# Moving the causal mask of a two-pass attention from TensorE to VectorE's maximum and to GpSimd's probabilities

## What is computed

```python
# x is (1, 2048, 512); 16 heads of 32
qkv = (x @ W_qkv + b_qkv).reshape(B, S, 16, 96).transpose(0, 2, 1, 3)
q, k, v = jnp.split(qkv, 3, axis=-1)
scores = jnp.einsum('bhqd,bhkd->bhqk', q, k) / np.sqrt(32)
scores = jnp.where(causal, scores, -10000.0)      # causal: key <= query
probs = jax.nn.softmax(scores, axis=-1)
ctx = jnp.einsum('bhqk,bhkd->bhqd', probs, v)
```

## Time and profile before

| | |
|---|---|
| median of three runs | 2159.66 us (2156.12 to 2161.9) |
| the profiled execution | 2161.04 us, span 2159.3 us |
| TensorE busy | 2000.4 us, 93% of the span |
| VectorE busy | 1098.8 us, 51% |
| ScalarE busy | 638.9 us, 30% |
| GpSimd busy | 436.7 us, 20% |
| mean granted TensorE clock | 0.956 |
| the attention block | from 195.3 us to about 873 us of the span |

### The profile page before, as it was taken

The page is one execution under the profiler, slowest core; times in us unless marked ns, Lnnn a source line. Parts: engine busy times, 40 slices in busy tenths (PEclk is TensorE's granted clock), DMA queues, the critical chain, the costliest instruction groups (busy, mean ns, idle before and its releaser), DMA issues. The chain is left out here.

```text
span 2159.3 us, 25676 instructions
## 1 busy us (share of the span) xinstructions
PE 2000.4 (93%) x10088; PEld 1415.3 (66%) x10088; DVE 1098.8 (51%) x1908; ACT 638.9 (30%) x1152; POOL 436.7 (20%) x385
## 2 busy tenths in 40 slices
PE   6997799999999999769999999997999869999998
PEld 4675444445444543557888888886887548888886
DVE  4452586677676760664434344334543674344334
ACT  3221144545545556231111111112321232111111
POOL 1124245756564345400000000000000300000000
PEclk9998599999999999979999999999999989999999
DMA  8625331151231100310000000002000002010002
GB/s 306 214 98 149 77 71 39 28 121 42 50 79 32 32 2 1 127 64 30 30 30 30 1 30 30 1 1 79 12 6 10 20 0 79 20 30 10 15 1 78
DMA packets 61720, 111.86 MB, mean 52 GB/s; under 512 B 6000, under 2 KB 21248, under 8 KB 61568
## 3 DMA queue, kind: packets, MB, share of 16 engines
q1 hardware_dynamic: 54144, 85.05, 14.0%
q0 software_dynamic: 7456, 25.18, 3.9%
HBM read 84.77 MB, written 25.44 MB: 51 GB/s over the span
## 5 line engine op out<-in xcount | busy, mean ns | idle before, releaser
L858 DVE TENSOR_REDUCE part_max<-banks 128x1 f32<-128x512 f32 (+2 forms) x640 | 356.4, 613 | 179.9 <-PE banks L734 109.0
L838 ACT ACTIVATE probs<-banks 128x512 f32<-128x512 f32 (+3 forms) x640 | 310.8, 538 | 362.0 <-PE banks L765 194.5
L734 PE MATMUL banks<-kst,qst 96*128 96x512 f32 (+2 forms) x640 | 276.0, 450 | 35.7 <-DVE part_max L858 20.2
L761 PE MATMUL banks<-qst,kst 98*128 98x512 f32 (+2 forms) x640 | 263.7, 423 | 13.9 <-DMA qst<-max_dram 12.3
L1312 DVE TENSOR_TENSOR tokens_a<-banks,tokens_a 128x512 f32<-128x512 f32 x224 | 151.6, 688 | 72.0 <-PE banks L216 70.3
L734 PEld LDWEIGHTS banks<-kst,qst 96*128 96x128 f32 x640 | 132.9, 210 | 82.3 <-DVE part_max L858 57.9
L761 PEld LDWEIGHTS banks<-qst,kst 98*128 98x128 f32 x640 | 125.8, 197 | 86.3 <-issue 54.1
L214 PE MATMUL banks<-h_hi,f_wg_hi 128*128 128x512 f32 x432 | 170.4, 395 | 12.1 <-DVE f_wg_lo L1276 12.1
L1337 DVE TENSOR_TENSOR tokens_b<-banks,tokens_b 128x512 f32<-128x512 f32 x64 | 44.3, 692 | 267.3 <-ACT tokens_b L1258 267.3
L214 PE MATMUL banks<-f_d_hi,f_hid_hi 128*128 128x512 f32 x432 | 171.1, 396 | 5.9 <-issue 3.6
L215 PE MATMUL banks<-h_lo,f_wg_hi 128*128 128x512 f32 x432 | 169.9, 393 | 0.0
(11 more groups left out here) (189 smaller groups left out, 3271.0 us busy)
## 6 DMA issues: line engine op xcount, KB each, us to landing
tokens_a<-in_L_wmod SPq DMA_DIRECT2D x12, 1024.0 KB, 6.9
qst<-q_hi SPq DMA_DIRECT2D x32, 256.0 KB, 5.9
kst<-k_hi SPq DMA_DIRECT2D x32, 256.0 KB, 8.4
tokens_b<-in_L_attn_x SPq DMA_DIRECT2D x4, 1024.0 KB, 13.2
q_hi<-qk_out_hi POOLq DMA_DIRECT2D x16, 256.0 KB, 3.4
q_lo<-qk_out_lo POOLq DMA_DIRECT2D x16, 256.0 KB, 3.4
k_hi<-qk_out_hi POOLq DMA_DIRECT2D x16, 256.0 KB, 3.1
k_lo<-qk_out_lo POOLq DMA_DIRECT2D x16, 256.0 KB, 3.4
```

The costliest lines, as they stand in the source:

```text
L734: mm = nc.tensor.matmul(dst[:, 0:wide], qst[0:BIASROW, n % QS, h, P * t:P * t + P], kst[0:BIASROW, (NB * g + c) % KS, h, 0:wide], start=Tr ...
L761: mm = nc.tensor.matmul(dst[:, c0:512], kst[0:BIASROW + 2, ck % KS, h, at:at + P], qst[0:BIASROW + 2, n % QS, h, c0:512], start=True, stop ...
L838: nc.scalar.activation(probs[:, q % PS, h, c0:512], bank[3 + sh % 3][:, c0:512], ACT.Exp, scale=SCALE).then_inc(exp_done, 1)
L858: nc.vector.tensor_reduce(part_max[:, n % 2, ht, c:c + 1], bank[slot % 3][:, 0:wide], AX_X, ALU.max).then_inc(max_read, 1)
```

## The change

The 512 mask matmuls are gone, and the bf16 tables with them. In the first pass, a diagonal max tile is reduced by one fused call that adds a mask `later` (SBUF, 640 columns, its window shifted by the tile) to the scores in place and keeps the maximum; it becomes two instructions on VectorE, the fused one and one that writes out the accumulator. In the second pass the later keys get whatever exponential they get, and GpSimd sets them to zero in `probs` with an affine select: 128 instructions of two heads by 128 columns, four a diagonal step. The context of a diagonal step waits for these. The butterflies of a pair are split, rounds 0 and 1 behind the first diagonal step's selects, rounds 2 and 3 and the store behind the second's. `later` is loaded on SyncE's queue behind the first pair's queries and keys (128 KB), and the load of constants at the start is 256 KB smaller.

```diff
                         wide = 512 if c < j else max(P * (t + 1), 2 * P)
-                        mm = nc.tensor.matmul(dst[:, 0:wide], qst[0:BIASROW, n % QS, h, P * t:P * t + P],
-                                              kst[0:BIASROW, (NB * g + c) % KS, h, 0:wide],
-                                              start=True, stop=(c < j))
-                        if c == j:
-                            at = P * t
-                            mw = 2 * P if t == 0 else P
-                            mm = nc.tensor.matmul(dst[:, at:at + mw], ident16[:], mask_queries[:, 0:mw],
-                                                  start=False, stop=True)
-                        mm.then_inc(max_mm, 1)
+                        nc.tensor.matmul(dst[:, 0:wide], qst[0:BIASROW, n % QS, h, P * t:P * t + P],
+                                         kst[0:BIASROW, (NB * g + c) % KS, h, 0:wide],
+                                         start=True, stop=True).then_inc(max_mm, 1)
...
-                        if t >= 0:
-                            mw = 2 * P if t == 3 else P
-                            mm = nc.tensor.matmul(dst[:, c0:c0 + mw], ident16[:], mask_keys[:, 2 * P - mw:2 * P],
-                                                  start=False, stop=True)
...
-                            pe.wait_ge(exp_done, 4 * q + 4)
+                            if diagonal:
+                                pe.wait_ge(masked, masks_before(s) + 2 * half + 2)
+                            else:
+                                pe.wait_ge(exp_done, 4 * q + 4)
...
-                        nc.vector.tensor_reduce(part_max[:, n % 2, ht, c:c + 1], bank[slot % 3][:, 0:wide], AX_X,
-                                                ALU.max).then_inc(max_read, 1)
+                        scores = bank[slot % 3][:, 0:wide]
+                        if c == j:
+                            at = P * (TB - 1 - t)
+                            nc.vector.tensor_tensor_reduce(out=scores, in0=scores, in1=later[:, at:at + wide], scale=1.0,
+                                                           scalar=LOWEST, op0=ALU.add, op1=ALU.max,
+                                                           accum_out=part_max[:, n % 2, ht, c:c + 1]).then_inc(max_read, 1)
...
+                    def mask(s):
+                        n, i = steps[s]
+                        for half in range(2):
+                            q, c0 = 2 * s + half, P * (2 * i + half - TB * (n % NB))
+                            for pair in range(2):
+                                pool.wait_ge(exp_done, 4 * q + 2 * pair + 2)
+                                here = probs[:, q % PS, 2 * pair:2 * pair + 2, c0:c0 + P]
+                                nc.gpsimd.affine_select(out=here, in_=here, pattern=[[0, 2], [1, P]],
+                                                        compare_op=ALU.is_ge, fill=0.0, base=0,
+                                                        channel_multiplier=-1).then_inc(masked, 1)
...
-                        elif i == 2 * (n % NB) and n in mixed_at:
-                            butterflies(mixed_at[n])
+                            continue
+                        mask(s)
+                        if n in mixed_at:
+                            butterflies(mixed_at[n], (0, 1) if i == 2 * (n % NB) else (2, 3))
...
+                    nc.vector.memset(later[:, 0:3 * P], 0.0).then_inc(later_ready, 1)
+                    dve.wait_ge(later_ready, 1)
+                    dve.wait_ge(later_loaded, 16)
```

More of the change, by code:

```diff
@@ L14 @@
 F32R = mybir.dt.float32r
-BF16 = mybir.dt.bfloat16
 ALU = mybir.AluOpType
@@ L35 @@
 MASKED = -32768.0
+LOWEST = -3.0e38
 BIASROW = 3 * HD
@@ L556, in build_program @@
             max_rows = sb(ctx, "max_rows", [2 * 4 * TB, 2, P], F32R)
+            later = sb(ctx, "later_keys", [P, 5 * P])
             turned_rec = sb(ctx, "turned_rec", [P, TB * 4])
@@ L565, in build_program @@
             ones_ready = sem(ctx, "ones_ready")
+            later_loaded = sem(ctx, "later_loaded")
+            later_ready = sem(ctx, "later_ready")
+            masked = sem(ctx, "masked")
             max_mm = sem(ctx, "max_mm")
@@ L632, in off_index, with masks_before @@
                 return off_before(n) + i
+            def masks_before(s):
+                return 4 * sum(not off_diagonal(q) for q in range(s))
             with nc.Block() as block:
@@ L660, in _ @@
                         load(n)
+                        if n == 0:
+                            sp.dma_start(later[:, 3 * P:5 * P], a["const"][:, 4 * P:6 * P]).then_inc(later_loaded, 16)
                     loads = [(quads_before(n - QS + 1), 1, n) for n in range(QS, NQ)]
@@ L679, in load_columns, with butterflies @@
                         pool.dma_start(fw[0], w2[:, :, cols]).then_inc(fw_loaded, 16)
-                    def butterflies(s):
+                    def mask(s):
[8 more added lines that the diff above has]
+                                                        channel_multiplier=-1).then_inc(masked, 1)
+                    def butterflies(s, rounds):
                         cols = slice(FW * s, FW * s + FW)
                         pool.wait_ge(fw_loaded, 16 * (s + 1))
-                        for r in range(4):
+                        for r in rounds:
                             half = 1 << r
@@ L690, in butterflies @@
                             pool.wait_ge(fw_step, 8 * s + 2 * r + 2)
-                        pool.dma_start(w2m[:, :, cols], fw[0]).then_inc(fw_stored, 16)
+                        if r == 3:
+                            pool.dma_start(w2m[:, :, cols], fw[0]).then_inc(fw_stored, 16)
                     def add_pair(s):
@@ L760, in score @@
                         ck, at = NB * g + kt // TB, P * (kt % TB)
-                        mm = nc.tensor.matmul(dst[:, c0:512], kst[0:BIASROW + 2, ck % KS, h, at:at + P],
-                                              qst[0:BIASROW + 2, n % QS, h, c0:512], start=True, stop=(t < 0))
-                        if t >= 0:
-                            mw = 2 * P if t == 3 else P
-                            mm = nc.tensor.matmul(dst[:, c0:c0 + mw], ident16[:], mask_keys[:, 2 * P - mw:2 * P],
-                                                  start=False, stop=True)
-                        mm.then_inc(score_mm, 1)
+                        nc.tensor.matmul(dst[:, c0:512], kst[0:BIASROW + 2, ck % KS, h, at:at + P],
+                                         qst[0:BIASROW + 2, n % QS, h, c0:512], start=True,
+                                         stop=True).then_inc(score_mm, 1)
                     def phase(s, half):
```

16 lines of the change are left out of this document (6 added, 10 removed).

## The result

| | before | after |
|---|---|---|
| median | 2160.62 us (2156.12 to 2163.59, 6 runs) | 2174.87 us (2169.73 to 2182.02, 6 runs) |
| profiled span, mean granted clock | 2159.3 us, 0.956 | 2179.6 us, 0.947 |
| ratio after / before | | 1.0071, 95% interval 1.0046 to 1.0096 |

The account below looks back on a forecast made before the run. TensorE was taken to bound the kernel, with VectorE right behind it in every burst with max tiles. The terms summed to -8.0 us, giving 2153.0 from the profiled run, 2151.6 from the median; 2152 was taken, range 2136 to 2170.

Parts of the forecast that it names:

- Items 1 to 5 of the sum: Attention bursts and the last 75 us: mask matmuls go, fused tiles cost VectorE more; -7.5, -1, 0 and +2, -3, -1 us.
- 4+4 diagonal burst: Fifteen diagonal bursts with 4+4 max tiles: each falls from 4.33 to 3.8 us, -7.5 us in all.
- larger diagonal ones: Fourteen diagonal bursts with 5+5 or more max tiles, already VectorE's: score masks go, tiles get dearer, -1 us in all.
- half-clock stretch: Stretch of 29.45 us at half clock, from 235 us: VectorE would end it at about 26.5 us, -3 us.
- bursts with fewer max tiles: Bursts without max tiles, and the last 75 us: ScalarE and contexts set the pace, only score masks go, -1 us.
- Off the diagonal: Bursts off the diagonal: 0 for 4+4 max tiles; +2 us for some 14 5+5 bursts that VectorE already decides.
- accumulator's write: Extra small VectorE instruction after each fused maximum: 0.08 us more per diagonal tile, at least 0, at most 0.20.
- Item 7: Program start: loading `later` costs +0.7 us, the smaller load of constants gives back -0.7 us.
- The first rival: VectorE sets the pace through dearer fused tiles and the kernel is slower: 2165 to 2176 us at 0.20 to 0.30; chance 0.13.
- Item 6: GpSimd: selects of 0.6 us, partly hidden, +1.5 us; two selects at the end, +1 us; store waits have 8 us cover.
- The third rival: Small VectorE chain collides more with GpSimd: a fifth more is +3 us, bad luck +12, 2164 us; chance 0.08.
- the clock's low stretches: Sign of being wrong: the prediction fails if the clock's low stretches move; no size given.

Follow-up runs that it names:

- loads_and_chain: Changed kernel with seven butterflies' loads reordered around selects and pair sums, and the small chain written as five reductions: 2138.35 us (0.9885).
- chain_before: Kernel before the change, with only its small chain on VectorE written as five reductions: 2143.93 us (0.9922).
- early_load: Changed kernel with the butterflies' loads of pairs 4 and 8 issued ahead of the selects of pairs 3 and 7: 2167.09 us (1.0033).
- second_pass_only: Kernel before with score masks replaced by GpSimd selects and butterflies split, max tiles keeping mask matmuls and plain reductions: 2180.95 us (1.0100).

## Why the prediction was wrong

The range ended at 2170, and 2174.87 us were measured.

*Items 1 to 5 of the sum, and 7.* The mechanism was right. The 4+4 diagonal burst takes 3.72 us (forecast 3.8), and the fifteen of them give -8.3 us in the pair of kernels without butterflies (forecast -7.5). The larger diagonal ones give -1.8 (forecast -1), the half-clock stretch takes 26.6 us (forecast 26.5), and the bursts with fewer max tiles give -1.3 (forecast -1). Off the diagonal the first two rows of the table give -0.2, and -1.6 in the pair of kernels with the chain of reductions, where I had forecast +2. The accumulator's write costs about 0.01 us (0.34 against 0.33), not 0.08; that dearer tiles were priced too high would explain the sign. Item 7 is as forecast: the first exponential starts at 235.8 us in both kernels. The first rival, VectorE as the pace, is out.

*Item 6, GpSimd, is the step that failed.* It priced the selects (0.41 us, forecast 0.6; the prediction's other figure, 0.22 without dispatch, was too low) and the contexts' waits for them. These are 6.9 us in the chain of waits in place of the "less than 3 us", and 3.4 once the loads are moved. The changed kernel's chain of waits (us in total, times, longest):

```profile
POOL tokens_b L682 <- DMA w_mixed<-tokens_b: 29.4, 5, 7.5
PE banks L751 <- DMA kst<-k_hi: 22.3, 3, 13.8
...
PEld banks L807 <- POOL probs L691: 6.9, 11, 2.1
```

The first line is 2.5 us more than in the kernel before. Of the second, 13.8 us are the wait for the first keys of the program, 13.3 before the change; the other two waits are new. What the item missed is the transfers between the selects. "The first waits for the butterflies' store, now late, fall in front of the next pair's pair sums, which have 8 us until they are used" was taken as nothing. The wait for the store is up to 7.5 us, it now ends after the scores already want their buffers back, and it cost steps 23, 24 and 44 (9.5 us in the table), and 43 too once the keys were in time. Moving those loads gave 23 us (2167.09 to 2144.01). That the load of pair 4 is itself an item in the queue behind the selects of pair 3, and so moves by 11 us into the load of the keys, isn't in the prediction at all; it is half of the 34.6 us of the table (8.8 and 8.2 in steps 22 and 42), though taking it away alone gave back only 7.8. This could be read before: the row at 417.31 stands 11 us ahead of SyncE's loads, and the order of GpSimd's queue shows the selects in between.

*The third rival, more collisions of the small chain,* had the right mechanism and a chance of 0.08. I counted selects as a fifth more GpSimd work. The runs point to something other than the amount, namely whether GpSimd has a backlog: the one new collision, of step 28, costs 6.4 us, where I had put a fifth more selects down as +3.

*The size of the gain where nothing else moves* was forecast as 8 us. It is 15.6 us by the medians without butterflies (10.9 in the table's attention row), and 16.1 with the loads moved. The items as measured above add up to about -14.5, against -10.5 forecast for items 1 to 5. On top of the chain of reductions it is 15.4 us in the attention row, but 5.6 by the medians: the five runs of loads_and_chain lie between 2130.6 and 2141.4 us, the profiled one is the quickest, and the four of chain_before lie within 1 us. Which of the two is nearer stays open. And the clock's low stretches did move, which the prediction had named as a sign of being wrong and had given no price.

## What to carry to other kernels

When a change puts waiting instructions into an in-order queue, list everything that stands behind them on that queue until its next free moment, and first of all the DMA issues: a load that used to run ahead in an idle gap now starts after the waits, beside whatever else starts then. Look for waits for a store ahead of work that others need, harmless ones too, since the change can move them onto the path; and move the load behind that work. And a chain of tiny copies on VectorE beside a busy GpSimd can be written with reductions: on the kernel before that alone gained 16 us, as much as the change of the mask gives once its queue is mended.

## What wasn't expected of the hardware

- A cast of 16 columns on VectorE took 7.97 us, through seven back-to-back tensor_tensors of GpSimd. Elsewhere in the same kernels a cast beside four such instructions took 0.8 us and the copy and subtraction behind it 1.2 and 1.3 us. What decides between them is open. The three longest casts (7.97 us here, 8.00 in early_load, 7.90 in second_pass_only) all met a GpSimd that had come out of a wait for a store with a backlog of twelve pair sums, and ended with the last of them. So did the one of 3.10 us at 342.52 us.
- A fused add and maximum that writes 256 columns back to its bank, with its accumulator's write, takes 0.34 us from start to start (0.61 for 512 columns), a reduction of 256 columns 0.33 (0.60).
- An affine select of 256 columns took 0.40 to 0.42 us in all 128 cases.
